# Four layer-1 steps in three-pass form, and an accumulating DMA as first level of the sum of products

## What is computed

```python
e = stack([tbl_f[ids[:, f]] for f in range(32)], axis=1)      # (512, 32, 32), indices b, field, d
prev = e
for W in (filter_0, filter_1):                                # 32*32 -> 128, then 32*128 -> 128
    z = einsum('bhd,bmd->bhmd', e, prev).reshape(b, h * m, d)
    prev = relu(einsum('bpd,pn->bnd', z, W[0]))
    outs.append(prev)
z = concatenate(outs, axis=1).sum(-1)                         # (512, 256)
h = concatenate([z, dense_ctx], axis=1)
h = maximum(h @ W_top1 + b_top1, 0); h = maximum(h @ W_top2 + b_top2, 0)
y = h @ W_top3
```

## Time and profile before

| | |
|---|---|
| Median of 3 runs | 946.62 us (946.28 to 947.04) |
| The profiled execution: its time, its span | 947.22 us, 945.3 us |
| TensorE busy | 881.0 us |
| VectorE busy | 765.0 us |
| ScalarE busy | 691.3 us |
| GpSimd busy | 773.2 us |
| Granted TensorE clock, mean over the span | 0.998 of full speed (full is 2.4 GHz) |

### The profile page before, as it was taken

One profiled execution on the slowest core, in us unless ns is written; L12 is line 12 of the kernel. 1 busy time (PEld: TensorE's weight loads), 2 busy tenths in 40 slices (PEclk: granted clock), 3 DMA queues, 4 the chain that ended last, 5 costly groups with the idle time before them and its releaser, 6 DMA issues.

```text
span 945.3 us, 17955 instructions
## 1 busy us (share of the span) xinstructions
PE 881.0 (93%) x3551; PEld 650.2 (69%) x3551; DVE 765.0 (81%) x2391; ACT 691.3 (73%) x2347; POOL 773.2 (82%) x582
## 2 busy tenths in 40 slices
PE   0289999999999999999999999999999999999989
PEld 0157777777777777777777777777777777777753
DVE  4068888889888888898888889988888899888893
ACT  2058777787878777878787778787877777877762
POOL 7768899888888999988889989887777877777772
PEclk9999999999999999999999999999999999999999
DMA  6031222222112222221122222211222222102000
GB/s 175 13 105 51 75 75 75 73 72 71 32 50 70 73 74 73 74 71 34 46 69 74 73 74 74 74 38 37 67 71 71 71 71 71 47 29 66 1 1 0
DMA packets 41436, 58.13 MB, mean 61 GB/s; under 512 B 7265, under 2 KB 16033, under 8 KB 41410
## 3 DMA queue, kind: packets, MB, share of 16 engines
q1 hardware_dynamic: 37314, 55.76, 18.6%
q0 software_dynamic: 4096, 2.11, 1.4%
HBM read 54.79 MB, written 3.05 MB: 61 GB/s over the span
## 4 chain that ended last, share of the span: by engine, by line
PE 53%; DVE 26%; issue 14%; POOL 4%; DVEq 2%; DMA 0%; ACT 0%
PE bank L836 38%; DVE acc L721 18%; PE bank L774 12%; POOL rows L331 4%; DVE pair L587 4%; DVE cur_low L598 2%; DVE parts L721 1%; DVEq L718 1%; PE bank L879 1%; DVEq L240 0%; PE bank L866 0%; PE bank L867 0%; DVE sum L629 0%; PE bank L874 0%; DVEq L707 0%
## 5 line engine op out<-in xcount | busy, mean ns | idle before, releaser
L521 ACT ACTIVATE parts<-bank,x 128x128 f32<-128x128 f32 x2048 | 584.8, 385 | 143.5 <-PE bank L836 140.1
L721 DVE SCALAR_TENSOR_TENSOR acc<-bank,x,acc 128x128 f32<-128x128 f32 x1792 | 485.6, 343 | 97.2 <-PE bank L836 96.0
L836 PE MATMUL bank<-w_high,cur_high 128*128 128x512 f32 x1024 | 440.5, 430 | 10.9 <-DVE acc L721 10.0
L836 PE MATMUL bank<-w_low,cur_high 128*128 128x512 f32 x1024 | 401.4, 392 | 0.0
L836 PE MATMUL bank<-w_high,cur_low 128*128 128x512 f32 x992 | 389.1, 392 | 0.0
L352 POOL TENSOR_TENSOR half<-parts 128x1024 f32<-128x1024 f32 x127 | 307.1, 2418 | 92.4 <-DVE parts L721 91.9
L836 PEld LDWEIGHTS bank<-w_high,cur_high 128*128 128x128 f32 x1024 | 192.5, 188 | 105.9 <-DVE acc L721 29.3
L836 PEld LDWEIGHTS bank<-w_low,cur_high 128*128 128x128 f32 x1024 | 193.0, 188 | 48.8 <-issue 14.8
L836 PEld LDWEIGHTS bank<-w_high,cur_low 128*128 128x128 f32 x992 | 186.4, 188 | 41.8
L352 POOL TENSOR_TENSOR half<-half 128x512 f32<-128x512 f32 x127 | 165.5, 1303 | 10.0
L378 POOL DMA_INDIRECT rows_next<-table_dram,ids_next x96 | 92.5, 963 | 17.5 <-issue 7.0
(11 more groups left out here) (77 smaller groups left out, 485.8 us busy)
## 6 DMA issues: line engine op xcount, KB each, us to landing
shifts<-x_scratch SPq DMA_DIRECT2D x155, 256.0 KB
x<-x_scratch SPq DMA_DIRECT2D x31, 256.0 KB, 2.9
x_scratch<-turned SPq DMA_DIRECT2D x31, 64.0 KB, 1.5
rows_next<-table_dram,ids_next POOLq DMA_INDIRECT x96
wt<-w_top_dram SPq DMA_DIRECT2D x2, 512.0 KB, 8.9
x_scratch<-turned SPq DMA_DIRECT2D x31, 32.0 KB, 1.8
rows<-table_dram,ids_sb POOLq DMA_INDIRECT x32, 2.4
w_sb<-w_ab_dram SPq DMA_DIRECT2D x1, 256.0 KB
```

What stands on the lines that cost most here:

```text
L521: ins = nc.scalar.activation(parts[q][ab][:, at:at + N2], act_bank[ab][:, i * N2:(i + 1) * N2], ACT.Copy, scale=x0[u][:, h, 2 * q + ab:2 * ...
L721: nc.vector.scalar_tensor_tensor(out=dst, in0=dve_bank[e % 2 * 2 + ab][:, i * N2:(i + 1) * N2], scalar=x0[u][:, h, 2 * q + ab:2 * q + ab + ...
L836: return nc.tensor.matmul(dst[:], cur_half[u][:, cols], w1_half[:, fields], **flags)
```

## The change

- `SPLIT` becomes (1, 2, 3, 4): steps 3 and 4 too are three fp32r products, with a rounding on ScalarE and a subtraction on GpSimd for each. `pair_low` becomes four tiles.
- The first level of the tree becomes a DMA issued from GpSimd, one for both tiles of a pair: it adds the right half of `parts` to the left half in SBUF (`add_halves`; 2 x 1024 columns on 128 partitions, 1 MB added to 1 MB). Just before it stands a tiny GpSimd instruction on `mark`. The issue waits until the pair's pieces are all written.
- GpSimd then waits for the DMA (`added`) and does the two levels that are left, one instruction each for both tiles (1024, then 512 columns). It also adds the two halves of `left` (`sum_left`, 512 columns). ScalarE applies ReLU on the way to x4_bank (`act_total`), VectorE only adds into sum2 (`dve_fold`, now at its slot 24); `dve_total` is gone.
- ScalarE's wait for parts is now for the first GpSimd level, so for the DMA and that instruction.
- Slots: `DVE_LOW16` 12 to 16, `ACT_HIGH16` 9 to 12, TensorE's products from 17, 19, 21, 23, 24 (steps 1, 3, 0, 4, 2) to 18, 19, 21, 22, 24 (steps 1, 2, 3, 0, 4), the turn of the fields a little earlier.
- GpSimd's order in a chunk: the low parts of steps 3 and 4, `add_halves` of q = 0, its gathers, `sum_parts`; then `add_halves` of q = 1, its gathers, the low parts of steps 1 and 2 of the chunk after, `sum_parts`, `sum_left`.

```diff
-TREE = 3
-LEFTS = 2
+TREE = 2
+LAST_TREE = 3
...
-SPLIT = (1, 2)
+SPLIT = (1, 2, 3, 4)
...
-ACT_PAIR_HIGH = {5: 1, 13: 2}
-ACT_HIGH16, DVE_LOW16 = 9, 12
-PE_PRODUCT = {17: 1, 19: 3, 21: 0, 23: 4, 24: 2}
+ACT_PAIR_HIGH = {4: 1, 8: 2, 9: 3, 16: 4}
+ACT_HIGH16, DVE_LOW16 = 12, 16
+PE_PRODUCT = {18: 1, 19: 2, 21: 3, 22: 0, 24: 4}
...
-ACT_TURN, PE_TURN, ACT_TURNED = 1, 6, 8
-
-ACT_LEFT, DVE_TOTAL, DVE_FOLD = 20, 24, 28
+ACT_TURN, PE_TURN, ACT_TURNED = 0, 4, 5
+
+ACT_TOTAL, DVE_FOLD = 20, 24
...
-            def sum_parts(chunk, pair_no, t):
...
-                for level in range(TREE):
...
-                    nc.gpsimd.tensor_tensor(dst, src[:, 0:width], src[:, width:2 * width],
-                                            ALU.add).then_inc(tree, 1)
...
+            def add_halves(pair_no, q, whole):
+
+                pool.wait_ge(act_prod, (pair_no + 1) * (2 * EACH))
+                pool.wait_ge(mac, (pair_no + 1) * (2 * MACS))
+                nc.gpsimd.tensor_tensor(mark[:], mark[:], mark[:], ALU.subtract)
+                n, width = slice(0, 2 if whole else 1), EACH * HG * N2 // 2
+                nc.gpsimd.dma_start(both_parts[q][:, n, 0:width], both_parts[q][:, n, width:2 * width],
+                                    accum_op=ALU.add).then_inc(added, 16)
+
+            def sum_parts(pair_no, q, whole):
+
+                n = slice(0, 2 if whole else 1)
+                pool.wait_ge(added, (pair_no + 1) * 16)
+                pool.wait_ge(tree, pair_no * TREE + 1)
+                nc.gpsimd.tensor_tensor(half[:, n, :], both_parts[q][:, n, 0:512], both_parts[q][:, n, 512:1024],
+                                        ALU.add).then_inc(tree, 1)
+                pool.wait_ge(tree, pair_no * TREE + 2)
+                nc.gpsimd.tensor_tensor(
+                    left[:, 2 * q:2 * q + n.stop, :, :].rearrange("p t l n -> p t (l n)"), half[:, n, 0:256],
+                    half[:, n, 256:512], ALU.add).then_inc(tree, 1)
+
+            def sum_left(chunk):
+
+                pool.wait_ge(tree, (chunk + 1) * (CPAIRS * TREE) + 1)
+                pool.wait_ge(total_rectified, chunk + 1)
+                nc.gpsimd.tensor_tensor(total.rearrange("p (t n) -> p t n", t=DC), left[:, :, 0, :], left[:, :, 1, :],
+                                        ALU.add).then_inc(totalled, 1)
...
+                for t in range(0, tiles, 2):
+                    whole = next_block or t < tiles - 2
                     if t % DC == 0 and (next_block or t < tiles - DC):
...
+                        pair_lows(k * CPB + t // DC + 1, (2, 3))
+                    add_halves(k * (tiles // 2) + t // 2, t // 2 % 2, whole)
+                    for s in (t, t + 1):
+                        if (next_block and s < rows_at) or (one_after and s > rows_at):
+                            for f in late[s]:
+                                gather(f)
+                    if t % DC == 2 and (next_block or t < tiles - DC - 2):
+                        pair_lows(k * CPB + t // DC + 2, (0, 1))
+                    sum_parts(k * (tiles // 2) + t // 2, t // 2 % 2, whole)
+                    if t % DC == 2 and whole:
+                        sum_left(k * CPB + t // DC)
...
+        def act_total(act, c, pairs_before):
+
+            act.wait_ge(totalled, c + 1)
             act.wait_ge(paired, pairs_before)
-            nc.scalar.copy(x4_bank[:].rearrange("p (t n) -> p t n", t=DC),
-                           left[u][:, :, 0, :]).then_inc(left_copied, 1)
+            nc.scalar.activation(x4_bank[:], total, ACT.Relu).then_inc(total_rectified, 1)
...
-                                    wait(act, tree, (pair_no - 2) * (2 * TREE) + ab * TREE + 1)
+                                    wait(act, tree, (pair_no - 2) * TREE + 2)
...
+        def dve_fold(dve, c, k):
+
+            dve.wait_ge(total_rectified, c + 2)
+            nc.vector.tensor_tensor(block_sum(k), x4_bank[:], block_sum(k), ALU.add).then_inc(folded, 1)
...
             if step == order[0]:
-                wait(pe, summed, c)
-                if turn:
-                    pe.wait_ge(turned_ready, c + 1)
-                if pair16_bank(c) is cur_bank:
-                    pe.wait_ge(low16, c + 1)
+                pe.wait_ge(low16, c + 1)
```

More of the change, by code:

```diff
@@ L114, in dlrm_tower @@
         acc = sb("acc", [P, 4, 2, N2])
-        parts = [[sb(f"parts_{i}{j}", [P, EACH * HG * N2]) for j in range(2)] for i in range(2)]
-        half = sb("half", [P, 1024 + 512])
+        both_parts = [sb(f"parts_{i}", [P, 2, EACH * HG * N2]) for i in range(2)]
+        parts = [[t[:, j, :] for j in range(2)] for t in both_parts]
+        half = sb("half", [P, 2, 512])
+        mark = sb("mark", [P, 1])
         sum2 = sb("sum2", [P, BLOCKS, DC, N2])
@@ L131, in dlrm_tower @@
         z1_half = free[:, (H1 + H2) // P * B:][:, 0:BLOCKS * 2 * P].rearrange("p (k h b) -> p k h b", k=BLOCKS, h=2)
-        lefts = free[:, 0:LEFTS * DC * 2 * N2].rearrange("p (i t l n) -> p i t l n", i=LEFTS, t=DC, l=2)
-        left = [lefts[:, i, :, :, :] for i in range(LEFTS)]
+        left = free[:, 0:DC * 2 * N2].rearrange("p (t l n) -> p t l n", t=DC, l=2)
+        total = free[:, DC * 2 * N2:DC * 3 * N2]
         z2, y_sb = pair[1], pair[0][0:1, 0:B]
@@ new lines, in block_body @@
+                    sum_parts(k * (tiles // 2) + t // 2, t // 2 % 2, whole)
+                    if t % DC == 2 and whole:
+                        sum_left(k * CPB + t // DC)
+                    for s in (t, t + 1):
+                        if next_block and s == rows_at:
+                            pool.wait_ge(gathered, (k + 1) * (F * 16))
+                            nc.gpsimd.tensor_copy(
+                                rows[:, bass.ds(k + 1, 1), :, :].rearrange("p o f d -> p (o f d)"),
+                                rows_next[:].rearrange("p f d -> p (f d)")).then_inc(rows_ready, 1)
+                            if one_after:
+                                fetch_ids(k + 2)
+                                pool.wait_ge(rows_ready, k + 2)
@@ L407, in _ @@
             pool.wait_ge(first_gathered[0], (F - LAST_TABLES) * 16)
             pool.wait_ge(first_gathered[1], LAST_TABLES * 16)
-            nc.gpsimd.memset(half[:, 0:1], 0.0).then_inc(rows_ready, 1)
+            nc.gpsimd.memset(half[:, 0, 0:1], 0.0).then_inc(tree, 1)
+            nc.gpsimd.memset(mark[:], 0.0).then_inc(rows_ready, 1)
+            pool.wait_ge(rows_ready, 1)
             fetch_ids(1)
@@ L412, in _ @@
                 gather(f)
-            pair_lows(1, (0,))
+            pair_lows(1, (0, 1))
             with pool.Fori(0, BLOCKS - 2) as k:
@@ L534, in body @@
                                     act_turn(act, c + 2)
-                                if slot == ACT_LEFT and not (first and u == 0):
-                                    act_left(act, c - 1, 1 - u,
-                                             CHUNKS * STEPS if last and u == UNROLL - 1 else (c + 2) * STEPS)
+                                if slot == ACT_TOTAL and not (first and u == 0):
+                                    act_total(act, c - 1,
+                                              CHUNKS * STEPS if last and u == UNROLL - 1 else (c + 2) * STEPS)
                                 if slot == ACT_X4 and not last:
@@ L683, in body @@
                                 dve_sum(dve, c)
-                            if slot == DVE_TOTAL and not (first and u == 0):
-                                dve_total(dve, c - 1, 1 - u)
                             if not (last and u == UNROLL - 1):
@@ L729, in _ @@
             src, width = parts[CPAIRS - 1][1], EACH * HG * N2 // 2
-            for level in range(TREE):
+            for level in range(LAST_TREE):
                 if level == 0:
@@ L847, in body @@
                                 if slot in PE_PRODUCT and not (last and u == UNROLL - 1):
-                                    pe_product(pe, c + 1, PE_PRODUCT[slot], turn=not last)
+                                    pe_product(pe, c + 1, PE_PRODUCT[slot])
                                 if slot == PE_TURN and not last:
```

94 lines of the change are left out of this document (27 added, 67 removed).

## The result

The changed kernel takes 994.29 us (median of 4 runs, 992.83 to 994.60) against 946.45 us for the kernel before in the same runs: a ratio of 1.0503, 95% interval 1.0485 to 1.0521. It is slower by 47.8 us where 15.4 were forecast. The direction is right and the time lies inside the range; the size is three times the forecast.

What follows compares the result with a forecast made beforehand. GpSimd's round of 27.4 us a chunk, just above TensorE's 27.3, was taken as the bound: (27.4 - 26.94) x 31 = 14.3, plus 1.0 at the end, is +15.3 on 947.22, a median of 962 us; range 945 to 999.

Steps and rivals of the forecast that it cites:

- Parts 1 and 2: Two more split steps save 0.32 us of the TensorE stretch; with the moved slots, the net is +11.2 us.
- The floor: VectorE stretch plus TensorE stretch of a chunk with the moved slots: 27.16 and 27.45 us, alternating.
- Part 3: GpSimd's in-order round per chunk: 12.6 us of work and gaps plus two transfers, 27.4 us.
- T: One accumulating transfer on GpSimd, issue to landing: taken as 7.4 us, fixed part 2.1 and data 5.3.
- Part 4: Kernel's start and end: nothing at the start, about +1 us at the end for the last pair's half-size transfer.
- (a): Transfer hidden, 7.3 us or less, so the moved slots decide: 958.8 us, range 954 to 962; chance 0.27.
- (b): Transfer much slower than two reads or colliding with loads: 999 us at 8.0, 1061 at 9; chance 0.15.
- (c): VectorE ends low16 by 13.3 us instead of 14.2, so faster: down to 26.3 us a chunk, 927; chance 0.16.
- (d): Edits cancel: low16 ends at 13.9 us instead of 14.2 and the transfer is hidden, 945 to 949 us; chance 0.10.

Runs made afterwards that it cites:

- quarter-size run: The changed kernel with a quarter of the columns in each accumulating transfer, three quarters of the first level left out: 960.53 us.
- split_only: The kernel before with the four split steps alone, its three-level tree and low16 slot kept: 977.57 us.
- reordered kernel with four split steps: The changed kernel with GpSimd's lows and sum_left reordered, old low16 and first-product slots, first chunk's low16 wait limited to step 0: 935.21 us, ratio 0.9863.
- the one with two: The changed kernel with only steps 1 and 2 split, old slots, GpSimd reordered likewise, no low16 wait in the first chunk: 934.89 us, ratio 0.9869.
- run with plain copies: The changed kernel with the same transfers as plain copies, overwriting the left half of parts instead of adding: 961.38 us.

## Why the prediction was wrong

**What bounds the kernel, right.** A chunk is a VectorE stretch ended by low16 and a TensorE stretch where GpSimd is out of the way: 14.49 and 12.76 us in the quarter-size run, for 14.46 and 12.70 forecast. In the changed kernel the TensorE stretch is the same 12.76, and the first one grows to 14.8 in the last block and to 15.1 and more before it, since ScalarE waits for parts in it. In the chunk that starts at 402.44 ScalarE waits 1.22 us for the first level, then TensorE 0.68 and VectorE 0.58 us for ScalarE. That is where GpSimd's round enters.

**Parts 1 and 2, right.** The floor was forecast at 27.16 and 27.45 and measured at 27.25 and 27.53 (quarter, copy), +12 us against +11.2. The 0.32 us of the two split steps is what `split_only` shows in its last block. TensorE idles 1.73 us ahead of the first product, of the 1.5 to 2 forecast, in this row of the changed kernel's timeline:

```profile
417.89 0.49 PE L778 MATMUL bank<-pair_high,w_high 128*128 128x512 f32 x1 [1.73 <-DVE pair_hl L604]
```

**Part 3, the mechanism right, the size wrong.** GpSimd's round was named as the bound, at 12.6 + 2 x 7.4 = 27.4 us. It is 11.56 of work and two transfers of 8.2 on average (8.3 beside gathers, 8.0 without), 28.0, and 0.2 more on average for what GpSimd does once a block: 28.19. The failed step is the term T, 7.4 forecast and 8.2 measured. The rows bounded it between 4.8 and 8.1, and the text chose 7.4: the fixed part at the low end, 2.1, and the data at 5.3, under the doubled 5.7, since rows of 4 KB should go faster than those of 2 KB. Quarter and full transfers, with no gathers beside them, start the next level 3.84 and 8.0 us after their issue. A line through the two gives 5.5 us for all the data and 2.5 us fixed (an estimate: by it the half-size transfer of the end would take 5.2, and it takes 4.65). So about half of the miss of 0.8 is in the fixed part, which came out near the gather's 2.4 and not at the 2.1 worked out from a store of SP. Some 0.2 is in the data, between the doubled 5.7 and the 5.3 taken, and 0.2 is what T grows beside the gathers, which the sum did not have.

Since T counts twice a chunk, 0.8 us of it is 50 us. That 1.0 us a chunk of this came back, 32 us in all, because the work around it is 11.6 and not 12.6 us (0.34 of it the two marks, at 0.13 and not 0.3 each, the rest small roundings up and gaps that are not there), is luck and not insight. By its own price of 62 us for each us of T, the text should have seen that its point hung on this one term, and that everything between 7.3 and 8.1 was one-sided: below 7.3 nothing is gained.

Of the miss of 32 us, 24 are this (28.19 against 27.4, 31 times). The start has 2.6 and the end 4.1, and the rest lies between the profiled executions and the medians.

**Part 4, wrong at both ends.** "The start is bound by the gathers: nothing" is wrong by 2.6 us. The diff drops a condition: before, the first chunk's first product did not wait for low16, since pair 16 of that chunk has a bank of its own; after, every chunk's does. TensorE's first product starts at 54.37 instead of 51.88, and 2.22 us of that is the wait for low16:

```profile
54.37 3.70 PE L778 MATMUL bank<-pair,w_sb 128*128 128x512 f32 x8 [2.22 <-DVE pair_hl L604]
```

With the condition back, the reordered kernel with four split steps starts its pitch line at 57.0, against 57.2 before; the one with two starts at 58.5, and the kernels without it start between 59.2 and 62.4, so runs differ here by a microsecond or more for other reasons too. The end was forecast at +1 us and is +5.1. GpSimd comes to the last pair late, since it is the bound: the last mac ends at 960.58, its issue is at 963.73 (timeline of GpSimd). The half-size transfer takes 4.6 us, near the 4.8 forecast. From the start of the last chunk to the end of the span the changed kernel takes 57.2 us against 52.1 before; both reordered kernels still take 56.7, and the run with plain copies 51.8. So this price belongs to the adding transfers, and not to GpSimd's late arrival alone. TensorE's filler ends and it idles:

```profile
963.73 0.89 POOL L346 DMA_DIRECT2D parts<-parts  x1
968.38 1.27 POOL L354 TENSOR_TENSOR half<-parts 128x512 f32<-128x512 f32 x1 [3.76 <-DMA parts<-parts]
```

```profile
972.81 0.47 PE L786 MATMUL bank<-ident,rows_next 128*128 128x128 f32 x1 [3.73 <-DVE rows_next L629]
```

**The rivals.** (a), the hidden transfer, is what the copy does: 961.4, forecast 958.8. (b) is what happened, in a mild form; at T = 8.0 it gave 999, near the 994 that was measured, but by terms that cancel: the work is 1.0 us a chunk less, and T, the start and the end are more. Its sign, ScalarE waiting for GpSimd at `parts`, came true with 69.8 us. (c) and (d) are excluded by the quarter-size run: even with short transfers the pitch is 27.35, above the 26.9 from which (c) decides, and the kernel is not faster.

## What to carry to other kernels

Before a step of an in-order engine is given to a DMA that the same engine issues and waits for, add up that engine's whole round, waits included, and ask what else it can do while the transfer runs; moving an operation under a transfer helps only if no engine waits for that operation, which has to be followed round the loop over the other engines. Where the sum hangs on a duration that no row shows, take the bad end of its bounds if only that side costs anything. And two bounds close to each other hide each other's price: measure each with the other taken away.

## What the runs showed of the hardware

An accumulating DMA is issued on GpSimd in 1.28 us, the same copy in 0.75 us (line 346, medians), against 0.97 for a gather in the earlier trace rows. While it runs the DMA engines are full (a share of 1 and above) at a much lower rate than the loads of the earlier trace rows, 197 GB/s against 322: one stretch of the changed kernel (PE, PEld, DVE, ACT, POOL busy, PEclk, DMA share, GB/s):

```profile
425.00:426.00 1.00, 1.00 (x6) 0.82 (x5) 1.00 (x5) 0.82 (x4) 0.00 (x0) 1.00 1.13 197
```

Other transfers beside it take longer. The 64 KB write of SP, which lands after 1.5 us in the earlier trace rows and again in the run with plain copies, takes three times as long in the changed kernel; nothing that waits for it was seen:

```profile
x_scratch<-turned SPq DMA_DIRECT2D x31, 64.0 KB, 4.8
```

At the end, TensorE's pause of 3.7 us is followed by a granted clock of half (1.2 GHz) and then full again, which the kernel before does not have at its end:

```profile
970.00:973.00 3.00, 0.19 (x2) 0.19 (x2) 2.10 (x4) 0.00 (x0) 0.45 (x1) 0.73 0.00 0
973.00:976.00 3.00, 3.00 (x7) 2.08 (x7) 0.00 (x0) 0.27 (x1) 0.00 (x0) 0.50 0.00 0
976.00:980.00 4.00, 4.00 (x8) 1.51 (x7) 0.00 (x0) 2.06 (x3) 0.00 (x0) 0.72 0.00 0
```

The time from the first transpose of the last block (line 786, 972.81) to the end of the span is 18.2 us, against 15.6 us before (929.74 to 945.3). In the quarter-size run the clock is 1.00 in this stretch, and it takes 15.6 us as well (943.09 to 958.7). In the reordered kernel with four split steps the clock reads 0.50 from 910 to 920, and it takes 17.0 us (917.02 to 934.0). So 2.6 of the 5.1 us at the end are the clock's, and not the transfer's directly. That the pause of 3.7 us is what lowers the clock is not shown: in the reordered kernel it reads 0.55 from 906 to 910, and TensorE's longest idle times of the 20 us before that are 1.33, 0.67 and 0.64 us.
